# Expert layer: norm groups of 2, 3 and 4 rows with centred down weights, addition ahead of each transfer, sorted rows loaded in pieces of 1, 1 and 2 tiles

## What is computed

```
logits = x @ w_router.T;  expert = argmax(logits);  score = sigmoid(logit of it)
shared = silu(x @ w_gate.T) * (x @ w_up.T) @ w_down.T
gate, up = split((score * x) @ gate_up_proj[expert])          # 2 x 256
out    = shared + (up * silu(gate)) @ down_proj[expert]
layernorm(x) = (x - mean(x)) / sqrt(var(x) + 1e-5)
```

## Time and profile before

| | |
|---|---|
| median of three runs | 344.0 us |
| the profiled execution | 344.77 us, of which the span of its instructions is 342.8 us |
| mean granted clock of PE | 0.933 of full speed |
| busy: PE, DVE | 269.8 us (79%), 286.7 us (84%) |
| busy: ACT, POOL | 186.5 us (54%), 192.5 us (56%) |
| output transfers, line 497 | 47, 996 ns each |

### The profile page before, as it was taken

One profiled execution on the slowest core, in us unless ns is written; L12 is line 12 of the kernel. 1 busy time (PEld: TensorE's weight loads), 2 busy tenths in 40 slices (PEclk: granted clock), 3 DMA queues, 4 the chain that ended last, 5 costly groups with the idle time before them and its releaser, 6 DMA issues. The chain is left out here.

```text
span 342.8 us, 6291 instructions
## 1 busy us (share of the span) xinstructions
PE 269.8 (79%) x1481; PEld 186.0 (54%) x1481; DVE 286.7 (84%) x1138; ACT 186.5 (54%) x573; POOL 192.5 (56%) x221
## 2 busy tenths in 40 slices
PE   3439999999998995839888888875999999998000
PEld 1215555555554552524555555543999888988000
DVE  6996999999999999996899988740389999999930
ACT  2524666656564652447666664203899888885000
POOL 5155777786776773300055556760007888888870
PEclk9987999999999999876999999999899999999755
DMA  6999900000000000000011111227940111110000
GB/s 190 376 424 391 409 8 0 2 3 0 2 0 2 2 0 0 0 2 2 0 63 64 63 62 64 95 78 238 354 158 24 31 35 37 40 36 30 26 2 0
DMA packets 13684, 28.39 MB, mean 83 GB/s; under 512 B 1966, under 2 KB 10166, under 8 KB 12626
## 3 DMA queue, kind: packets, MB, share of 16 engines
q1 hardware_dynamic: 10464, 21.57, 17.2%
q0 software_dynamic: 3040, 6.37, 5.5%
q10 hardware_dynamic: 146, 0.07, 0.1%
HBM read 15.38 MB, written 13.60 MB: 85 GB/s over the span
## 5 line engine op out<-in xcount | busy, mean ns | idle before, releaser
L452 POOL TENSOR_TENSOR kv<-qk,vv 128x1024 f32<-128x1024 f32 x32 | 62.4, 1950 | 2.5
L1025 PE MATMUL banks<-kv,upto 128*128 128x512 f32 x128 | 62.6, 612 | 1.3 <-POOL kv L452 1.3
L1164 PE MATMUL banks<-xsT,w_now 128*128 128x128 f32 x376 | 52.6, 284 | 0.3 <-DVE hT_e L964 0.3
L497 POOL DMA_INDIRECT out<-rows,token_i x47 | 46.8, 996 | 9.9 <-issue 8.3
L446 POOL TENSOR_TENSOR qk<-ex,rl 128x256 f32<-128x256 f32 x32 | 23.3, 727 | 47.2 <-ACT ex L553 47.2
L1164 PEld LDWEIGHTS banks<-xsT,w_now 128*128 128x128 f32 x376 | 47.1, 197 | 0.9 <-issue 0.6
L479 POOL DMA_INDIRECT sorted_rows<-rows,slot_i x32 | 31.7, 990 | 25.8 <-DVE slot_i L821 17.7
L735 DVE TENSOR_TENSOR prod<-banks,qk 128x1024 f32<-128x1024 f32 x32 | 38.9, 1216 | 3.5 <-PE banks L1025 2.9
L757 DVE TENSOR_REDUCE num<-prod 128x128 f32<-128x1024 f32 x32 | 38.6, 1207 | 0.3 <-DVE den L752 0.3
L964 DVE TENSOR_TENSOR hT_e<-silu_e,banks 128x256 f32<-128x256 f32 x47 | 19.3, 412 | 18.8 <-ACT silu_e L640 15.3
L1044 PE MATMUL banks<-w_qkvo,xnT 128*128 128x384 f32 x64 | 28.7, 532 | 8.1 <-ACT xnT L535 3.9
(11 more groups left out here) (161 smaller groups left out, 647.8 us busy)
## 6 DMA issues: line engine op xcount, KB each, us to landing
sorted_rows<-rows SPq DMA_DIRECT2D x3, 1950.0 KB, 13.4
rows<-sorted_rows SPq DMA_DIRECT2D x10, 520.0 KB, 6.3
w_exp<-in_gate_up SPq DMA_DIRECT2D x4, 1024.0 KB, 20.3
w_exp_down<-in_down SPq DMA_DIRECT2D x4, 512.0 KB, 20.4
rows<-in_x SPq DMA_DIRECT2D x1, 1024.0 KB, 11.0
rows<-sorted_rows SPq DMA_DIRECT2D x2, 390.0 KB, 4.7
rows<-in_x SPq DMA_DIRECT2D x1, 768.0 KB, 8.2
out<-rows,token_i POOLq DMA_INDIRECT x47
```

The lines of the kernel that those rows point to most:

```text
L452: nc.gpsimd.tensor_tensor(kv[:, u, :].rearrange("p (h m d) -> p h m d", h=NH, m=HD), k, v, ALU.mult).then_inc(s_kv, 1)
L497: nc.gpsimd.indirect_dma_start(out=out_rows, out_offset=bass.IndirectOffsetOnAxis(ap=token_i[:, j - 1:j], axis=0), in_=rows[:, j - 1, 0:D] ...
L1025: ins = nc.tensor.matmul(ps_s[u % 2][:, cols], upto[:], kv[:, u, cols], start=True, stop=True)
L1164: ins = nc.tensor.matmul(ps_gue[u % 2][:, c * P:(c + 1) * P], w_now[:, u % 2, c * P:(c + 1) * P], xsT[:, u % 2, :], start=True, stop=True)
```

## The change

The mean over a token's 128 values is taken out of the down weights: multiplied with `I - 1/128` (`centring`) they yield products without a mean, so shared output and expert output have none, and the norm needs only the variance. This is done in the kernel: the weights are loaded the other way round, and PE multiplies them with `centring`, which turns and centres them; DVE copies the shared ones, ACT those of the experts, two experts at a time, in the place of the unused matmuls, of which one stays.

- The norm steps become `scale_steps`, eleven per group, without the two for the mean and one for the shift. Groups are of rows 0-1, 2-3, 4-5, 6-8, 9-11 and then four each, 44 to 46 last.
- Between the large instructions of a tile step stand one, or in the first groups two, norm steps. Rows are scaled in place, as soon as their group is ready; `yn` is gone. Statistics are taken in the tile step of their sum.
- Token numbers are made in two instructions (`tokens`), not one per four rows.
- POOL adds rows 0 to 33; rows 34 to 46 are scaled and added by DVE in one instruction.
- Loads: tile 0, tile 1, tiles 2-3, then four tiles each. ACT's `xsT` copy of tile 0 stands ahead of `xs` of tile 1.

```diff
+def scale_steps(nc, series, st, width, scratch, rs):
+    mean_even, sq_even, sq_odd = st
+    ve, y, t = scratch
+    yield series.done(tensor(t, mean_even, mean_even, ALU.mult))
+    yield series.done(fused(out=ve, in0=sq_even, scalar=width * EPS, in1=sq_odd, op0=ALU.add, op1=ALU.add))
...
+    yield series.done(fused(out=rs, in0=t, scalar=0.5625, in1=y, op0=ALU.add, op1=ALU.mult))
+SCALE_STEPS = 11
-        ADDED_BY_POOL = 4 * (QUADS - 2)
+        ENDS = [2, 4, 6, 9, 12] + list(range(16, ST, 4)) + [ST]
+        LOADED = [1, 2, 3, 3] + [j // 4 + 3 for j in range(4, ST)]
+        ADDED_BY_POOL = 34
@@ sync
-            pieces = [(0, 1), (1, 4)] + [(q, min(q + 4, ST)) for q in range(4, ST, 4)]
+            pieces = [(0, 1), (1, 2), (2, 4)] + [(q, min(q + 4, ST)) for q in range(4, ST, 4)]
@@ gpsimd
-                    if g == NG - 1:
-                        pool.sem_inc(s_last_scatters, 1)
-                    nc.gpsimd.tensor_tensor(r, r, yn[:, j % 4, :], ALU.add).then_inc(s_fin, 1)
+                    nc.gpsimd.tensor_tensor(x1, x1, flat(rows[:, j:j + 1, D:2 * D]), ALU.add).then_inc(s_fin, 1)
+                    if j - 1 in (0, TOKENS_FIRST):
+                        pool.wait_ge(s_token, 1 + (j > 1))
@@ scalar
+            for n in range(E // CENTRED_AT_ONCE):
+                act.wait_ge(s_turned_e, n + 1)
+                nc.scalar.copy(w_exp_down[:, CENTRED_AT_ONCE * n:CENTRED_AT_ONCE * (n + 1), :, :].rearrange(
+                    "p e c d -> p (e c d)"), ps_centred[n % 3][:]).then_inc(s_centred_e, 1)
@@ vector, setup
+            nc.vector.tensor_tensor(centring[:], ident[:], neg_mean[:], ALU.add).then_inc(s_centring, 1)
...
+            dve.wait_ge(s_turned_d, 1)
+            nc.vector.tensor_copy(w_d[:].rearrange("p c d -> p (c d)"), ps_s[1][:, 0:FC * D]).then_inc(s_centred_d, 1)
@@ vector, experts
+            def scale_row(i):
+                dve.wait_ge(s_series3, SCALE_STEPS * (GROUP_OF[i] + 1))
+                if i < ADDED_BY_POOL:
+                    nc.vector.tensor_scalar(r, r, rstd3[:, i:i + 1], None, ALU.mult).then_inc(s_yn, 1)
+                else:
+                    nc.vector.scalar_tensor_tensor(out=x1, in0=r, scalar=rstd3[:, i:i + 1], in1=x1,
+                                                   op0=ALU.mult, op1=ALU.add).then_inc(s_fin_last, 1)
+            for j in range(-2, ST + 1):
+                many, most = begun in (1, 2, 3), begun == 1
+                    nc.vector.tensor_tensor(hT_e[:, u % 2, :], silu_e[:, u % 2, :], ps_gue[u % 2][:, F:2 * F],
+                                            ALU.mult).then_inc(s_he, 1)
+                chain_steps(1 + many)
...
+                    nc.vector.tensor_tensor(r, ps_ye[u % 2][:, 0:D], r, ALU.add).then_inc(s_sum, 1)
+                chain_steps(1 + most)
+                if scaled < ST and begun > GROUP_OF[scaled] + (left > 0):
+                    scale_row(scaled)
+                    scaled += 1
+                if scaled == 1:
+                    scale_row(scaled)
+                    scaled += 1
+                chain_steps(1 + many)
...
+                    nc.vector.bn_stats(stats3[:, j, :], r).then_inc(s_stats3, 1)
+                chain_steps(1 + most)
+                if begun < len(GROUPS) and j + 1 == GROUPS[begun][1]:
+                    chain_steps(left)
+                    chain, left, begun = scales(begun), SCALE_STEPS, begun + 1
+                    chain_steps(1)
@@ tensor
+                if t == 0:
+                    pe.wait_ge(s_centring, 1)
+                    pe.wait_ge(s_w2, 16)
+                    for c in range(FC):
+                        ins = nc.tensor.matmul(ps_s[1][:, c * D:(c + 1) * D], w_down[:, c * P:(c + 1) * P], centring[:],
+                                               start=True, stop=True)
+            def centre(n):
+                pe.wait_ge(s_wexp, 16 * (E // 4) * 2)
+                at_least(pe, s_centred_e, n - 2)
+                for k in range(CENTRED_AT_ONCE * FC):
+                    e, c = CENTRED_AT_ONCE * n + k // FC, k % FC
+                    ins = nc.tensor.matmul(ps_centred[n % 3][:, k * D:(k + 1) * D], w_exp_out[:, e, c * P:(c + 1) * P],
+                                           centring[:], start=True, stop=True)
+            centre(0)
+            centre(1)
             nc.tensor.matmul(ps_turn[0:1, 0:P], tile_rank[:], ident[:], start=True, stop=True).then_inc(s_tile_row, 1)
-            for n in range(GT + 2):
-                if 0 < n <= GT:
-                    pe.wait_ge(s_last_scatters, n)
...
-                for _ in range(1 if 0 < n <= GT else 2):
-                    nc.tensor.matmul(ps_idle[:], ident[:], w_g_u[:, 0:4 * P], start=True, stop=True)
+            for n in range(2, E // CENTRED_AT_ONCE):
+                centre(n)
+            pe.wait_ge(s_scattered, 16 * NT)
+            nc.tensor.matmul(ps_idle[:], ident[:], w_g_u[:, 0:4 * P], start=True, stop=True)
```

More of the change, by code:

```diff
@@ L619, in step3, with turned @@
                 j = 4 * q + u
+                def turned():
+                    if live(j + 3, ST):
+                        act.wait_ge(s_xs_t, j + 4)
+                        at_least(act, s_gue, j + 2)
+                        nc.scalar.copy(xsT[:, (u + 1) % 2, :], ps_xs[:, 0:D]).then_inc(s_xsT, 1)
+                if j == -3:
+                    turned()
                 if live(j + 4, ST):
@@ new lines, in scales @@
+            def scales(g):
+                c = slice(*GROUPS[g])
+                norm = Series(dve, s_series3, SCALE_STEPS * g)
+                dve.wait_ge(s_stats3, GROUPS[g][1])
+                yield from scale_steps(nc, norm, [stats3[:, c, k] for k in (1, 2, 5)], D,
+                                       [scratch3[:, k, c] for k in range(3)], rstd3[:, c])
+            def scale_row(i):
+                x1, r = flat(rows[:, tiles(i), 0:D]), flat(rows[:, tiles(i), D:2 * D])
+                dve.wait_ge(s_series3, SCALE_STEPS * (GROUP_OF[i] + 1))
[4 more added lines that the diff above has]
+                                                   op0=ALU.mult, op1=ALU.add).then_inc(s_fin_last, 1)
@@ new lines, in tokens, with chain_steps @@
+            def tokens(j0, j1):
+                dve.wait_ge(s_loaded, LOADED[j1 - 1])
+                nc.vector.tensor_scalar(token_i[:, j0:j1], rows[:, j0:j1, TOKEN], -1.0, float(NTOK), ALU.mult, ALU.add
+                                        ).then_inc(s_token, 1)
+            begun, scaled = 0, 0
+            chain = iter(())
+            left = 0
+            def chain_steps(count):
+                nonlocal left
+                for _ in range(count):
+                    if left:
+                        next(chain)
+                        left -= 1
@@ L981, in step3 @@
                     nc.vector.tensor_tensor(r, ps_ye[u % 2][:, 0:D], r, ALU.add).then_inc(s_sum, 1)
[L982 to L1000 removed]
+                chain_steps(1 + most)
[6 more added lines that the diff above has]
+                chain_steps(1 + many)
+                if j == 0:
+                    tokens(0, TOKENS_FIRST)
+                if j == TOKENS_REST:
+                    tokens(TOKENS_FIRST, ST)
+                if live(j, ST):
+                    dve.wait_ge(s_sum, j + 1)
+                    nc.vector.bn_stats(stats3[:, j, :], r).then_inc(s_stats3, 1)
[4 more added lines that the diff above has]
+                    chain_steps(1)
+            while scaled < ST:
+                if begun > GROUP_OF[scaled] + (left > 0):
+                    scale_row(scaled)
+                    scaled += 1
+                chain_steps(2)
         @block.tensor
```

132 lines of the change are left out of this document (56 added, 76 removed).

## The result

| | before | after |
|---|---|---|
| median | 344.05 us (4 runs, 342.65 to 344.68) | 338.56 us (4 runs, 337.88 to 339.72) |
| the profiled execution | 344.77 us, span 342.8 us | 337.88 us, span 336.1 us |
| mean granted clock of PE | 0.933 | 0.920 |

The ratio is 0.985, with a 95% interval of 0.981 to 0.989: the change makes the kernel 5.5 us faster. Forecast were 8.3 us and a median of 335.7. The time lies in the range of 333.6 to 340.0, but above the forecast's own narrower one (334.5 to 337.2). By the profiled executions the last transfer ends 6.8 us earlier (327.96 against 334.74), not 8.3.

The account below looks back on a forecast made before the run. POOL's queue was taken to set the end: 8.3 us from an earlier start and 2.2 from six fewer additions, less 1.7 for gaps and 0.5 for start-up, gave 8.3 us off 344.77, then 0.8 to the median: 335.7 us, range 333.6 to 340.0.

Parts of the forecast that it names:

- What bounds the kernel: Expert stage: POOL's unbroken queue of additions and transfers sets the end, 1.66 us a round, then 1.294 us a transfer.
- Rival A: Expert stage: DVE stays the bound, waits for POOL eat the saved steps, tiles stay at 1.71 us; 339.9 us, chance 0.13.
- rival B: POOL's early queue: no gaps, tiles pass at 1.44 us and POOL is fed from row 3 on; 333.6 us, chance 0.12.
- Rival C: POOL's queue: POOL's additions are held by DVE's scaling, 0.33 us each, making the kernel slower; 346.9 us, chance 0.06.
- Rival E: Expert stage's start: it gains nothing, load or centring late by 1 to 2 us; 337 to 338 us, chance 0.05.
- The start of the stage: Expert stage's start: separate load of tile 1 and ACT's new order bring the first product 1.2 us earlier (0 to 1.5).
- The gaps: POOL's queue, rows 2 to 12: waits for DVE's scaling take back 1.7 us of the earlier start.
- DVE idle from 275 on: Expert stage: a sign that DVE should have idle time from 275 us on, which it had not before.
- Centring: Wait for scattered rows: 9.0 us of PE matmuls and ACT's copies are hidden, cost 0, with 0.5 us of cover left.
- Rival D: Expert stage's start: PE's clock at 1.2 GHz for four more tiles, start 3 to 5 us later; 339 to 341, chance 0.04.
- Start-up: Start of the kernel: two more DVE instructions, centring matrix and copy of shared weights, cost +0.5 us (0.2 to 0.7).
- From the profile to the median: Whole kernel: the median of the runs is taken as 0.8 us below the profiled execution, turning 336.5 into 335.7 us.

Follow-up runs that it names:

- loads_back: Changed kernel with sorted rows loaded in pieces of 1 and 3 tiles and ACT's start order as before: 341.60 us against 340.54 for the changed kernel.
- pool_adds_12: Changed kernel with POOL making 12 additions in place of 34 and DVE the other 35: 351.63 us, ratio to the kernel before 1.014.
- warm_twice: Changed kernel with two warming matmuls behind the landing of the rows in place of one: 340.39 us against 346.95 before, ratio 0.981.

## Why the prediction was right, and where it was off

*What bounds the kernel: right for the kernel after, not quite for the one before.* POOL's queue sets the end. Its length repeats within 0.2 us, and six more additions cost 2.15 us. In the kernel before it wasn't quite a queue that never waits: POOL waited 1.74 us ahead of its second addition, and later four transfers took 6.82 us and not 4 x 1.66 = 6.64, which is DVE's 1.71 a tile:

```profile
287.63 1.00 POOL L497 DMA_INDIRECT out<-rows,token_i  x1 [0.25 <-issue]
...
294.45 1.00 POOL L497 DMA_INDIRECT out<-rows,token_i  x1 [0.25 <-issue]
```

So the faster tiles also gave some 0.05 us for each of these rows. Rival A fell (1.52 to 1.56 us a tile, not 1.71), rival B too (gaps came). Rival C fell: the additions take 0.44 to 0.49 us, and from row 13 on no round is over 1.67. It is DVE that is held. Rival E came in part: the start gained, but the first transfer was late by 0.9 us all the same, for the reasons given under the start and the landing. The Trainium skill (SBUF — State Buffer, "Who interferes with whom") has an instruction of DVE with two SBUF inputs contend with a GpSimd instruction that reads SBUF; instructions of DVE that take two to three times as long where POOL has additions agree with it in kind (the longest hold was of a scaling, a tensor_scalar with one such input, which the section has contend only in some modes; that this one ran in such a mode no row shows), and its "Issue order, not op shape, decides who blocks" would let POOL be held as well, of which no row here shows anything.

*The start of the stage: mis-sized.* The 1.2 us for loads and ACT's order measured 0.93 in the profiled pair, of which `loads_back` returns 0.27 to 0.56 beside the changed kernel of its own group. The wait of 1.26 us in the earlier trace rows was 0.71 and 0.87 in other executions of the same kernel. A wait for a transfer, read from one execution, is one draw.

*The landing: not in the sum.* In the profiled execution the scatters landed 0.76 us later than before's. With the 0.27 missing from the loads, less 0.16 us that the stretch from the first product to the first transfer was shorter than forecast, that makes the first transfer 0.9 us late.

*The gaps: mis-sized.* From the first transfer to the addition of row 12 I had 271.3 - 250.1 = 21.2 us; it took 21.86. From there to the end forecast (325.9 - 271.3) and trace (327.96 - 273.36) both have 54.6. 0.9 and 0.66 make up the 1.56 us.

*DVE idle from 275 on: wrong.* At 6.05 us of work for four tiles that pass at 1.51 us each nothing is left over, so this sign contradicted my own sum. DVE's work without holds is shorter (1.29 us a tile in `pool_adds_12`), but where POOL adds, the holds fill the difference. The pace came out right since I took the price per step with its waits in it.

*Centring: hidden, as forecast; the warming matmul beside it had a price that I left out.* PE and ACT were done before the landing. What cost time was that only one warming matmul stayed behind the landing: with a second one PE's clock did not fall, and the first transfer came 0.65 to 1.0 us earlier (`warm_twice`). In the pair of the forecast both kernels spent 3.4 us at half clock, so this is no part of the 1.56 us. Rival D had the mechanism, but its price of 3 to 5 us was too large: tiles are limited by ACT and DVE too, and 3.4 us at half clock cost under one.

*Start-up: right at its place (0.72 us at the carry in the profiled pair, 0.57 as means), not found in the total.* Without the shared part the median is the same, within some 2 us.

*From the profile to the median: wrong.* I took 0.8 us off, as before's profiled execution lay above its median. After's lay 0.7 below: 1.45 us of the 2.9 us by which the median was missed.

By the traces, from the load's issue to the end, the change gains 101.01 - 93.62 = 7.4 us as means of three each, and 8.1 us in the pair of the forecast. The medians gain less: 5.5, 6.9 and 5.0 us in the three groups, 5.8 on average. So 1.6 us are missing, and still 0.7 if before's stage took its shortest time, 100.15 us, in every execution. The start-up can account for 0.5. The traces can't settle the rest: before's three profiled executions lay 0.7, 2.4 and 3.2 us above the medians beside them and after's 0.4 to 1.2 us below, and their loads were issued at 233 to 239 us. Whether the change costs time ahead of the stage stays open.

## What to carry to other kernels

Where one engine's queue ends the kernel, forecast that queue entry by entry, from its first entry to its last: it repeated to 0.2 us. But take the waits for transfers and the clock at its start from several executions. When a change drops work that "does nothing", ask what it kept going: here it was PE's clock. And a full timeline may be waits for a shared resource: take the other user away before calling an engine the bound.

## What the hardware showed that was not expected

- By the trace, the end of PE's work reached ACT and DVE late, by up to 3.7 us, while POOL issued indirect transfers 1.29 us apart in the expert stage. With an addition between them (1.66 us) this did not happen in any trace, nor beside the scatters of routing. The two kernels with 12 and 16 additions came out 11 and 10 us slower than `warm_twice`. The cause is open.
- PE's clock fell to 0.50 in eight of eight traces with 1.13 us of work behind the landing (for 3.4 us, in one for 6.8), and in two of six with 1.98 us. PE's next work came 2.6 to 2.8 us after the landing in all.
- The kernel before issued its first load at 233.05, 237.07 and 238.17 us in three traces, on three chips: the same code ahead of the stage differs by 5 us, more than most terms of the forecast. Some 3 us of that lie in routing: from the first scatter to the first of the last four it takes 53.31, 55.43 and 56.16 us.
